# Two graph-attention layers on Trainium2: more layer-1 masks on VectorE, guards dealt out around them, and layer 0's mask pieces moved earlier in ScalarE's turn

## What is computed

```python
def _L0_gnn_ref(data, connectivity, W, b, src_proj, trg_proj):      # 8 heads of 64
    data1 = (data @ W.T + b).reshape(N, H, D)
    src = jnp.einsum('nhd,xhd->nh', data1, src_proj)
    trg = jnp.einsum('nhd,xhd->nh', data1, trg_proj)
    e = src.T[:, :, None] + trg.T[:, None, :]
    e = jnp.where(e >= 0, e, 0.01 * e) + connectivity[None, :, :]
    scores = jax.nn.softmax(e, axis=-1)
    return jnp.einsum('hnm,hmd->hnd', scores, ...)                  # back to N x 512

def _L1_gnn_ref(node_matrix, adjacency_matrix, Wks, Wqs, Wvs, Wo):  # 8 heads of 64
    adj = jnp.maximum(adjacency_matrix, jnp.eye(n))
    atts = jnp.einsum('hqk,hmk->hqm', queries, keys) / key_dim ** 0.5
    atts = atts - 1e+16 * (1.0 - adj)[None, :, :]
    atts = jax.nn.softmax(atts, axis=-1)
    return jnp.einsum('hqm,hmk,hko->qo', atts, values, Wo)

h = jnp.maximum(_layernorm(x), 0.0);  x = x + _L0_gnn_ref(h, adj, ...)
h = jnp.maximum(_layernorm(x), 0.0);  x = x + _L1_gnn_ref(h, adj, ...)
```

## Time and profile before

| | |
|---|---|
| median of 3 runs | 4676.87 us (4674.9 to 4680.1) |
| the profiled execution | 4677.4 us, span 4675.6 us |
| granted TensorE clock, mean | 0.978 |
| TensorE busy, matmul / weight load | 4440.1 us (95%) / 2137.3 us (46%) |
| VectorE / ScalarE / GpSimd busy | 3542.8 (76%) / 3246.9 (69%) / 3434.2 (73%) us |
| layer-1 low parts, L1398 GpSimd | 2048 x 1171 ns |
| layer-1 guards, L1488 VectorE | 2112 x 689 ns |
| layer-1 masks on VectorE, L1577 | 512 x 691 ns |
| layer-1 masks on TensorE, L1635 | 1536 x 379 ns |
| layer-0 row masks, L733 ScalarE | 256 x 716 ns |

### The profile page before, as it was taken

How to read it: one execution, slowest core, us unless ns; L and a number is a source line. 1 busy time by engine, 2 the same in 40 slices (tenths; PEclk the granted TensorE clock), 3 DMA queues, 4 the chain that set the end, 5 groups by cost and what they waited for, 6 DMA issues and landing times. The chain is left out here.

```text
span 4675.6 us, 112897 instructions
## 1 busy us (share of the span) xinstructions
PE 4440.1 (95%) x43276; PEld 2137.3 (46%) x43276; DVE 3542.8 (76%) x7470; ACT 3246.9 (69%) x6022; POOL 3434.2 (73%) x2955
## 2 busy tenths in 40 slices
PE   8699999999999978969999999999999999999998
PEld 4222222222222224416556655656655566556555
DVE  5498998988989843367777777777777777777776
ACT  5366666666666633318878878878878788788786
POOL 2476676676776720029989989989989899899897
PEclk9899999999999989969999999999999999999999
DMA  3566776676676533353333433433423334334333
GB/s 143 131 210 196 202 224 201 204 211 208 206 213 184 169 112 112 106 174 86 111 112 92 127 101 90 127 101 99 124 83 111 112 93 130 98 88 127 103 102 102
DMA packets 462941, 646.14 MB, mean 138 GB/s; under 512 B 49536, under 2 KB 271104, under 8 KB 452288
## 3 DMA queue, kind: packets, MB, share of 16 engines
q1 hardware_dynamic: 383968, 522.36, 37.7%
q10 hardware_dynamic: 73856, 100.83, 6.8%
q0 software_dynamic: 4576, 15.73, 1.2%
HBM read 528.38 MB, written 110.38 MB: 137 GB/s over the span
## 5 line engine op out<-in xcount | busy, mean ns | idle before, releaser
L1398 POOL TENSOR_TENSOR d_PL<-d_PF,d_PH 128x512 f16<-128x512 f32 x2048 | 2324.3, 1171 | 296.0 <-ACT d_PH L1448 293.1
L1488 DVE CUSTOM_DVE_ANT_0 d_junk<-d_gd,d_MR 128x512 bf16<-128x512 f32 x2112 | 1441.9, 689 | 500.4 <-issue 465.3
L1444 ACT ACTIVATE d_PF<-d_sc 128x512 f32<-128x512 f32 x2048 | 1283.1, 627 | 518.4 <-DVE d_sc L1577 317.2
L1448 ACT ACTIVATE d_PH<-d_sc 128x512 f16<-128x512 f32 x2048 | 1292.3, 631 | 0.0
L809 DVE SCALAR_TENSOR_TENSOR b_P<-R,u,b_A 128x512 f32<-128x512 f32 x1792 | 1195.3, 738 | 108.8 <-PE b_den L867 58.8
L860 PE MATMUL b_acc<-b_P,V 128*64 128x512 f32 x4096 | 967.7, 608 | 77.8 <-DVE b_P L809 38.3
L1616 PE MATMUL d_gd<-d_KA,d_QA 128*128 128x512 f16 x2112 | 815.6, 387 | 60.6 <-DMA d_KA<-scratch_kl 30.6
L1632 PE MATMUL d_sc<-d_QA,d_KA 128*128 128x512 f16 x2048 | 776.8, 379 | 2.1 <-DVE d_QL L1501 2.1
L1633 PE MATMUL d_sc<-d_QL,d_KB 128*128 128x512 f16 x2048 | 776.3, 379 | 0.0
L1653 PE MATMUL d_acc<-d_V,d_PH 128*128 128x65 f16 x8192 | 638.9, 192 | 2.9 <-ACT d_PH L1448 0.2
L1655 PE MATMUL d_acc<-d_V,d_PH 128*128 128x64 f16 x8192 | 639.9, 193 | 0.0
(11 more groups left out here) (133 smaller groups left out, 4352.7 us busy)
## 6 DMA issues: line engine op xcount, KB each, us to landing
d_V<-scratch_v SPq DMA_DIRECT2D x131, 520.0 KB, 4.6
stage<-in_adjT SPq DMA_DIRECT2D x128, 512.0 KB, 4.5
b_srow<-in_adj ACTq DMA_DIRECT2D x256, 256.0 KB, 5.0
b_rows<-in_adj SPq DMA_DIRECT2D x112, 512.0 KB, 6.6
d_MR<-scratch_mr SPq DMA_DIRECT2D x36, 1024.0 KB, 5.4
d_MT<-scratch_mt SPq DMA_DIRECT2D x35, 1024.0 KB, 6.3
d_KA<-scratch_kh SPq DMA_DIRECT2D x272, 128.0 KB, 3.0
d_KA<-scratch_kl SPq DMA_DIRECT2D x272, 128.0 KB, 3.2
```

Of the source, the lines that this page charges most:

```text
L1398: eng.tensor_tensor(PL[:, t % H_RING, :], PF[:, t % F_RING, :], PH[:, t % H_RING, :], ALU.subtract).then_inc(s_lowp if by_pool(t) else s_l ...
L1444: nc.scalar.activation(PF[:, t % F_RING, :], sc[(nb * TILES + t) % BANKS][:, :], ACT.Exp, scale=EXP_SCALE)
L1448: nc.scalar.activation(PH[:, t % H_RING, :], sc[(nb * TILES + t) % BANKS][:, :], ACT.Exp, scale=EXP_SCALE).then_inc(s_P, 1)
L1488: nc.vector.tensor_tensor_reduce(out=junk[:, gi % 2, :], in0=gd[gi % 2][:, :], in1=MR[:, s, c * QB:(c + 1) * QB], scale=1.0, scalar=-3.0e3 ...
```

## The change

In layer 1, `masked_by_vector` now holds for every second tile in round 0 and for tiles 3, 5 and 7 of each eight in rounds 1 to 3: 104 of 256 tiles, before 64. The guards are dealt over steps 1 to 28: two per step, three in every fourth step (4, 8, ..., 28) and in step 14. The diagonal set-up moves from step 6 of round 2 to step 29 of it, the four diagonal pieces to steps 30 and 31 of round 2 and 0 and 3 of round 3. In layer 0, the store of piece m-1 and the load of piece m+1 are issued in `move_rows`, right after the two exponentials of step m; loads and stores have one semaphore per buffer place, so a store no longer waits for the store ahead of it. Three semaphores of layer 1 are merged into others.

```diff
-            def mask_row(nb, par, j):
-
-                n = nb * PIECES + j
+                act.dma_start(piece("mr", n), mrow[:, n % 2, :]).then_inc(s_mr[n % 2], 16)
+
+            def move_rows(n):
+
                 if n:
                     store_row(n - 1)
-                act.wait_ge(s_srow, 16 * (n + 1))
                 if n + 1 < NB * PIECES:
                     load_row(n + 1)
+
+            def mask_row(nb, par, j):
+
+                n = nb * PIECES + j
+                act.wait_ge(s_srow[n % 2], 16 * (n // 2 + 1))
                 if j == 0:
                     act.wait_ge(s_lim, nb + 1)
                 if n >= 2:
 
-                    act.wait_ge(s_mr, 16 * (n - 1))
+                    act.wait_ge(s_mr[n % 2], 16 * (n // 2))
...
                 for m in range(NT):
                     exp_adj(nb, m, first)
+                    move_rows(nb * PIECES + m)
                     max_lifted(nb, half, par, m)
...
-    FIRST_G, LAST_G = 2, 28
+    FIRST_G, LAST_G, EXTRA_G = 1, 28, 14
...
+    def guard_count(mb):
+        if not FIRST_G <= mb <= LAST_G:
+            return 0
+        return 3 if mb % 4 == 0 or mb == EXTRA_G else 2
+
     def guards_of(mb):
-        def upto(step):
-            return GUARDS * min(max(step - FIRST_G + 1, 0), LAST_G - FIRST_G + 1) // (LAST_G - FIRST_G + 1)
-        return range(upto(mb - 1), upto(mb))
+        first = sum(guard_count(k) for k in range(mb))
+        return range(first, first + guard_count(mb))
...
-    DIAG_STEP, SETUP_STEP = (HP - 2) * NT + 1, (HP - 2) * NT + 6
-    ROW_SET = [free + 4 for free in ROW_FREE]
+    DIAG_STEP, SETUP_STEP = (HP - 2) * NT + 1, (HP - 1) * NT - 3
+    ROW_SET = [(HP - 1) * NT + late for late in (-2, -1, 0, 3)]
...
     def masked_by_vector(t):
-        return t % 4 == 3
+        return t % 2 == 1 if t < PAIR else t % 8 in (3, 5, 7)
```

More of the change, by code:

```diff
@@ L470, in layer0_attention @@
         s_lim = sem("limits_negated")
-        s_srow = sem("sign_rows_in")
+        s_srow = [sem(f"mask_piece_in{i}") for i in range(2)]
         s_ms = sem("row_masks")
-        s_mr = sem("row_masks_stored")
+        s_mr = [sem(f"row_masks_stored{i}") for i in range(2)]
         s_rm = sem("row_limit")
@@ L593, in _ @@
             sp.wait_ge(s_md, 16 * SUB * NB)
-            sp.wait_ge(s_mr, 16 * PIECES * NB)
+            for i in range(2):
+                sp.wait_ge(s_mr[i], 16 * PIECES * NB // 2)
         @block.gpsimd
@@ L710, in load_row @@
                     act.wait_ge(s_ms, n - 1)
-                act.dma_start(srow[:, n % 2, :], piece("adj", n)).then_inc(s_srow, 16)
+                act.dma_start(srow[:, n % 2, :], piece("adj", n)).then_inc(s_srow[n % 2], 16)
             def store_row(n):
                 act.wait_ge(s_ms, n + 1)
-                act.wait_ge(s_mr, 16 * n)
-                act.dma_start(piece("mr", n), mrow[:, n % 2, :]).then_inc(s_mr, 16)
+                act.dma_start(piece("mr", n), mrow[:, n % 2, :]).then_inc(s_mr[n % 2], 16)
+            def move_rows(n):
+                if n:
+                    store_row(n - 1)
+                if n + 1 < NB * PIECES:
+                    load_row(n + 1)
             def mask_row(nb, par, j):
                 n = nb * PIECES + j
-                if n:
-                    store_row(n - 1)
-                act.wait_ge(s_srow, 16 * (n + 1))
-                if n + 1 < NB * PIECES:
-                    load_row(n + 1)
+                act.wait_ge(s_srow[n % 2], 16 * (n // 2 + 1))
                 if j == 0:
@@ L1166, in layer1_attention @@
     P_SHIFT = math.log(4096.0) / EXP_SCALE
+    def guard_count(mb):
+        if not FIRST_G <= mb <= LAST_G:
+            return 0
+        return 3 if mb % 4 == 0 or mb == EXTRA_G else 2
     def guards_of(mb):
-        def upto(step):
-            return GUARDS * min(max(step - FIRST_G + 1, 0), LAST_G - FIRST_G + 1) // (LAST_G - FIRST_G + 1)
-        return range(upto(mb - 1), upto(mb))
+        first = sum(guard_count(k) for k in range(mb))
+        return range(first, first + guard_count(mb))
+    assert sum(guard_count(mb) for mb in range(NT)) == GUARDS
     ROW_FREE = [(HP - 2) * NT + next(m for m in range(NT) if 2 * MC * (s + 1) - 1 in guards_of(m)) + 1 for s in range(SUB)]
-    DIAG_STEP, SETUP_STEP = (HP - 2) * NT + 1, (HP - 2) * NT + 6
-    ROW_SET = [free + 4 for free in ROW_FREE]
+    DIAG_STEP, SETUP_STEP = (HP - 2) * NT + 1, (HP - 1) * NT - 3
+    ROW_SET = [(HP - 1) * NT + late for late in (-2, -1, 0, 3)]
     POOL_SLOTS = (0, 1, 2, 3)
@@ L1266, in layer1_attention @@
         s_m1 = sem("misc1_read")
-        s_rd = sem("reciprocal")
-        s_oN = sem("normalised")
-        s_x = sem("x1_in")
+        s_oN = sem("inverted_normalised")
+        s_x = sem("const_and_x1_in")
         s_out = sem("out_stored")
@@ L1314, in _ @@
         def _(sp):
-            sp.dma_start(idh[:, :], DR["idh"]).then_inc(s_const, 16)
-            sp.dma_start(xr[:, :, :], DR["Wo"].rearrange("(c p) n -> p c n", p=P)).then_inc(s_const, 16)
+            sp.dma_start(idh[:, :], DR["idh"]).then_inc(s_x, 16)
+            sp.dma_start(xr[:, :, :], DR["Wo"].rearrange("(c p) n -> p c n", p=P)).then_inc(s_x, 16)
             load_diagonals(sp, 0)
@@ L1415, in _ @@
         def _(act):
-            act.wait_ge(s_const, 16 * 2)
+            act.wait_ge(s_x, 16 * 2)
             act.wait_ge(s_set, 2)
@@ L1526, in add_rows @@
                 if s == 0:
-                    dve.wait_ge(s_x, nb * 16 + 16)
+                    dve.wait_ge(s_x, nb * 16 + 48)
                 dve.wait_ge(s_m1w, nb * M1_USES + (HP + s + 2))
@@ L1551, in _ @@
             copy_crows(0, 0)
-            dve.wait_ge(s_const, 16 * 2)
+            dve.wait_ge(s_x, 16 * 2)
             dve.wait_ge(s_set, 3)
@@ L1695, in _ @@
                 guard(0, 0, gi, 0, 0)
-            pe.wait_ge(s_const, 16 * 2)
+            pe.wait_ge(s_x, 16 * 2)
             crow(0)
```

9 lines of the change are left out of this document (4 added, 5 removed).

## The result

The changed kernel takes **4600.99 us** (median of 4 runs, 4598.45 to 4603.38) against 4678.42 us of the kernel before (4674.9 to 4680.1): ratio **0.9838** (95% interval 0.9826 to 0.985), 77 us less. 4599 us was forecast. The profiled execution took 4598.45 us, its span is 4596.6. The total is right; the experiments show that several terms of the sum are not.

The account below looks back on a forecast made before the run. Layer 1 was taken as bound by the number of TensorE matmuls, layer 0 by TensorE with a few holes. 4677.4 - 69 - 15 + 7 + 8 - 9 = 4599 us; range 4581 to 4645.

Parts of the forecast that it names:

- Matmuls removed, −69: Layer 1: 320 mask matmuls fewer on TensorE at 0.215 us each, all on the engine setting the pace: -69 us.
- VectorE's added work, +7: Layer 1: 320 more mask operations, hidden except in steps 1 to 7; 0.8 us per block, +7 us, bounds 0 and 48.
- The guards' dealing, taken as 0: Layer 1: the number of guards stays 64 a round; no term in the sum for their new order.
- Set-up, −15 and +8: Layer 1: moving the diagonal set-up from step 6 of round 2 gains 15 us; its new place costs 8 us.
- Layer 0, −9: Layer 0: earlier loads and stores let the adj chunk be issued earlier, VectorE waits 2 us less: -9 us, bounds -12 and +5.
- nothing changes there: Layer 0's largest TensorE hole, the wait for ScalarE's accumulator copies (5.41, then 5.90 in place of 3.65 us), would stay.
- no gap: Layer 0: the issues of loads and stores fall under ScalarE's second exponential, so they cost no time.
- GpSimd's pace: Layer 1 rival: GpSimd's low parts set the pace, 2.33 us a step against TensorE's 2.24: 4642 us, chance 0.13.
- VectorE late in each round: Layer 1 rival: upper bounds of both VectorE terms, 48 and 15 in place of 7 and 8: 4647 us, chance 0.10.
- rival 2: Layer 1: VectorE late in each round, TensorE waiting for guards in steps 1 to 9: 4647 us, chance 0.10.
- ScalarE paying for masks: Layer 1 rival: ScalarE's wait for each VectorE mask finds no slack, 2.53 us per masked step: 4794 us, chance 0.04.
- The Trainium skill's rule: Layer 1 rival: TensorE has room by its weight-load share, so removed matmuls gain nothing: 4653 us, chance 0.03.

Follow-up runs that it names:

- layer 0 alone: The kernel before with only the changed layer 0 (earlier loads and stores, semaphores per buffer place) and the merged semaphores: 4672.17 us, ratio 0.9995.
- the kernel with every second tile: The changed kernel with every second tile masked by VectorE in all four rounds, 24 masks a block more: 4584.99 us, ratio 0.9789.
- The masks alone: The kernel before with only the new masked_by_vector, guards and set-up as before: 4671.16 us, ratio 0.9992.
- guards alone: The kernel before with only the new dealing of guards: 4650.82 us, ratio 0.9947.
- set-up back: The changed kernel with the diagonal set-up and its pieces back at their old places (step 6 of round 2): 4638.34 us, ratio 0.9904.
- the guards at the ends: Every second tile by VectorE, but TensorE masks steps 0, 2, 30, 31; one guard each in steps 0 and 29, from 14 and 28: 4581.48 us, ratio 0.9794.

## Why the prediction was right, and where it was not

The rounds forecast as 84.6, 75.6, 76.2 and 75.9 us came out as 85.4, 75.5, 75.65 and 75.3: 311.8 us a block where 312.3 was forecast. That layer 1 is bound by TensorE's matmuls over most of a round is right. The total holds because errors of both signs met, and that is luck: 17 us too much from the matmuls, 11 to 14 too little for VectorE and some 7 too much in layer 0, against 24 to 28 us from the guards' dealing that no term held and some 5 more from the set-up.

- **Matmuls removed, −69.** The count and the price per matmul are right, and TensorE is what bounds the steps with guards. The step that failed is "all on the engine that sets the pace": in the guardless steps ScalarE does. Measured with nothing put in their place: −50 to −52.
- **VectorE's added work, +7 (bounds 0 and 48).** Mis-sized: it is +18 to +21, inside the bounds. It shows in the guard wait, 2.2 us a block without the work and 11.1 with it. My steps 1 to 7 ended one step too early; most of it falls in step 8.
- **The guards' dealing, taken as 0.** The failed step that matters most: I checked that the guards stay 64 a round and asked no further. It is −24 alone. I had seen TensorE lose "about 0.6 us by the rhythm of the rows" and did not ask what the new rhythm does to it. By most blocks' lengths, guards first, then set-up, then masks: 320.9, 317.4, 316.0, 311.8, times 8: −28, −12 and −34.
- **Set-up, −15 and +8.** Alone −10 to −12, near the 7 net. With the new masks it is −31. I had priced it in the kernel before, where VectorE has more slack behind it than it would have with the masks added.
- **Layer 0, −9.** ScalarE's wait for pieces went, as said: 23.9 us in place of 177.8. The step that failed is that VectorE's wait for the chunk would shrink with it: it did not halve, 4.42 us after 4.45 (3.52 in the run with layer 0 alone), since the chunk's loads, issued earlier, are reached earlier too. The whole brought some 2 us, not told from none. At the place of which I had said "nothing changes there" the wait for the accumulator copies was 4.71 to 5.91 us in seven blocks, 36.9 in total, and is 4.97 or 4.98 in each, 34.9 in total; but the seven product stretches behind it take 42.3 us and not 38.2, so nothing was gained there. And "no gap" was wrong: the operation behind the two issues (L688) stands for "issue" 21 times, 15.9 us in total over layer 0, where mask_row (L733) stood so for 10.2 us before.
- **Rivals.** GpSimd's pace is refuted for this dose: with 93% busy it still waited 24 us a block for ScalarE, and the kernel with every second tile is faster still. VectorE late in each round is half true, with 21 us, which the guards gave back. VectorE's lateness is in rival 2's place, behind the turned copies. ScalarE paying for masks is refuted as a mechanism by its wait of 37.9 us for 84 masks. The Trainium skill's rule in "Perfetto Trace Analysis", section "Identifying the Most-Contended Engine", by which weight loads at 192 of 320 us leave TensorE room, would have made the removed matmuls worthless. The masks alone gave almost what that says, and for another reason: with no VectorE work in their place the same matmuls gave about 50 us, so here the trace disagrees with the rule as I had used it. I had used half of it: the section names MFU, the share of the peak rate that the matmuls reach, beside the weight loads. An estimate of that share from the rows, a block's matmul columns at 0.215 us per 512, is about 300 of 321 us, which leaves little room and agrees with the trace.

Four things stay open. The new masks bring 4 to 6 us with the old dealing and the old set-up, 11 by the blocks with the new dealing and the old set-up (guards alone to set-up back, 317.5 to 316.2 us a block on average), and 31 to 34 with both new; the steps where TensorE stands are read from the traces above, but no run changed one of them alone. Why the old dealing and the set-up leave two lengths of round 2 (78.7 and 80.4, 79.7 and 81.1) isn't known. Whether layer 0 gains anything isn't known, since traces of the same code differ by more. What the guards at the ends gain over every second tile is below what these runs can tell.

## What to carry to other kernels

A bound changes from step to step inside one loop: count what a removed instruction is worth only in the steps where its engine really sets the pace, which the gaps between starts on each engine's timeline show. What a long operation costs depends on its engine's slack behind it (10 us for the set-up before the masks were added, 31 after), so price it in the kernel as it will be, not as it is. When a change re-deals work "evenly" without changing its amount, work out the idle time that the old deal left, since that may be the larger part; and take parts out of the full change as well as putting each in alone, since here the parts alone sum to 42 us and together give 76. Before a gain of a few us in one stretch is believed, look at the same stretch in other traces of the same code: here layer 0's attention differs by 6 us between them.

## What the runs showed of the hardware

ScalarE's DMA issue is not always short. The issue of a mask piece's load (L712) takes 0.44 us at 752.52 and at 771.56 us, but 1.30 us at 758.48 and 1.85 us at 764.89, towards the end of and after SP's issue of R's eight loads, and ScalarE's next operation waits 0.72 and 1.18 us for it ("issue" in the row above). SP's own issue of a `stage` load takes 1.87 us at 759.30 and 0.38 at 772.29. A busy DMA share alone isn't the cause: it is 1.00 from 760 to 765 us, with 165 GB/s moved, and 1.06 from 770 to 775, with 398 GB/s, where the issue is short again. What is behind it was not looked for. And one VectorE operation of 1.6 us took 4.43, once, in one trace of the changed kernel:

```profile
3634.12 4.43 DVE L1522 TENSOR_TENSOR d_oR<-d_oC,d_rd 128x512 f32<-128x512 f32 x1
```

Its round 0 took 90.0 us in place of 85.4. The cause was not looked for.
